# Mixture-of-experts layer with gathered conditioning: a low part on Pool, ranks ahead of a transpose, half a batch of the shared projection kept for later, and the last rows split over two engines

## What is computed

```python
h  = einsum('bsi,bio->bso', x, W[id]) + b[id][:, None, :]     # per batch its own 256x256 matrix
y  = (silu(h @ sw1) * (h @ sw3)) @ sw2                        # shared expert, 352 wide
scores = softmax(h @ gate_w)                                  # 8 experts, the best 2 kept
for e in range(8):                                            # routed experts, 176 wide
    y += weight[:, e] * ((silu(h @ rw1[e]) * (h @ rw3[e])) @ rw2[e])
return x + y
```

## Time and profile before

| | us |
|---|---|
| median of 3 runs | 119.95 (119.51 to 120.24) |
| the profiled execution's own time | 120.04 |
| its span in the profile | 118.4 |
| PE busy | 106.3 |
| DVE busy | 67.8 |
| ACT busy | 52.2 |
| Pool busy | 46.1 |

### The profile page before, as it was taken

The page is one execution under the profiler, slowest core; times in us unless marked ns, Lnnn a source line. Parts: engine busy times, 40 slices in busy tenths (PEclk is TensorE's granted clock), DMA queues, the critical chain, the costliest instruction groups (busy, mean ns, idle before and its releaser), DMA issues.

```text
span 118.4 us, 2226 instructions
## 1 busy us (share of the span) xinstructions
PE 106.3 (90%) x624; PEld 90.0 (76%) x624; DVE 67.8 (57%) x221; ACT 52.2 (44%) x131; POOL 46.1 (39%) x62
## 2 busy tenths in 40 slices
PE   6887997706999999899999999999999999999791
PEld 4676886404678888667799989999999997888570
DVE  1044575037984199867878676577655543024951
ACT  4035575117161693255657755346555655103000
POOL 4360077730776200001653443443453635704400
PEclk9999999965699999999999999999999999999999
DMA  3899999998886257131223343241012110029843
GB/s 72 237 298 276 345 352 371 383 324 226 216 194 235 89 158 201 41 96 48 91 95 106 100 130 119 86 136 59 29 44 83 50 67 21 0 55 383 329 184 118
DMA packets 16737, 19.08 MB, mean 161 GB/s; under 512 B 2338, under 2 KB 13718, under 8 KB 16726
## 3 DMA queue, kind: packets, MB, share of 16 engines
q1 hardware_dynamic: 13302, 12.62, 35.5%
q0 software_dynamic: 1984, 4.46, 10.7%
q10 hardware_dynamic: 1440, 1.86, 4.7%
HBM read 12.64 MB, written 7.21 MB: 168 GB/s over the span
## 4 chain that ended last, share of the span: by engine, by line
PE 73%; DMA 8%; issue 6%; another core or an unknown queue 3%; POOL 3%; DVE 2%; ACTq 1%; ACT 1%; POOLq 1%; DVEq 0%
PE bank L846 52%; DMA y_area<-_out_by_choice_and_token 6%; PE bank L858 6%; PE bank L978 4%; PE bank L1013 4%; DMA _out_by_choice_and_token<-y_area,dest 2%; PE bank L876 2%; PE bank L873 1%; ACTq L306 1%; POOL _out_by_choice_and_token L406 1%; PE bank L875 1%; POOLq L287 1%; POOL cond_area L288 1%; POOL ids_bc L365 1%
## 5 line engine op out<-in xcount | busy, mean ns | idle before, releaser
L406 POOL DMA_INDIRECT _out_by_choice_and_token<-y_area,dest x23 | 23.6, 1025 | 40.7 <-DVE y_area L767 26.4
L394 POOL DMA_INDIRECT rows_by_expert<-h_area,slot x16 | 15.5, 971 | 15.9 <-DVE slot L628 11.6
L846 PE MATMUL bank<-w_all,hsT_hi 128*128 x72 | 21.6, 342 | 0.0
L846 PE MATMUL bank<-hT_area,sh_area 128*128 128x512 f32 (+1 forms) x72 | 18.7, 421 | 0.0
L846 PEld LDWEIGHTS bank<-hT_area,sh_area 128*128 128x128 f32 (+1 forms) x72 | 13.7, 193 | 4.2
L846 PEld LDWEIGHTS bank<-w_all,hsT_hi 128*128 128x128 f32 x72 | 13.0, 188 | 0.0
L761 DVE TENSOR_TENSOR y_area<-y_area,bank 128x176 f32<-128x176 f32 x23 | 7.7, 335 | 8.5 <-ACT y_area L503 4.3
L503 ACT ACTIVATE y_area<-bank 128x176 f32<-128x176 f32 x23 | 7.3, 318 | 10.1 <-PE bank L846 8.2
L846 PE MATMUL bank<-w_all,hsT_lo 128*128 x36 | 11.5, 320 | 0.0
L846 PE MATMUL bank<-raw,gT_f 88*128 x44 | 11.3, 378 | 0.0
L546 DVE TENSOR_TENSOR hsT_lo<-bank,hsT_hi 128x256 fp32r<-128x256 f32 x18 | 7.6, 423 | 6.3 <-ACT hsT_hi L499 5.5
(11 more groups left out here) (128 smaller groups left out, 198.2 us busy)
## 6 DMA issues: line engine op xcount, KB each, us to landing
h_area<-rows_by_expert SPq DMA_DIRECT2D x23, 128.0 KB
raw<-in_L_ffn_rw_dram SPq DMA_DIRECT2D x16, 176.0 KB
raw<-in_L_ffn_rw_dram SPq DMA_DIRECT2D x2, 704.0 KB
rows_by_expert<-x_area SPq DMA_DIRECT2D x8, 128.0 KB
y_area<-_out_by_choice_and_token SPq DMA_DIRECT2D x4, 256.0 KB, 4.4
y_area<-_out_by_choice_and_token ACTq DMA_DIRECT2D x4, 256.0 KB, 5.1
out_dram<-x_area SPq DMA_DIRECT2D x3, 256.0 KB, 2.1
sh_raw<-in_L_ffn_sw_dram SPq DMA_DIRECT2D x2, 352.0 KB, 5.0
```

The costliest lines, as they stand in the source:

```text
L394: nc.gpsimd.indirect_dma_start(out=rows_dram, out_offset=bass.IndirectOffsetOnAxis(ap=slot[:, i, t:t + 1], axis=0), in_=h_sb[:, t, :], in_ ...
L406: nc.gpsimd.indirect_dma_start(out=y_dram, out_offset=bass.IndirectOffsetOnAxis(ap=dest[:, j:j + 1], axis=0), in_=y_sb[j % NBY], in_offset ...
L846: last = nc.tensor.matmul(dst, w, v, start=start and n == 0, stop=stop and n == len(operands) - 1)
```

## The change

- Pool makes the low part of the shared weights' first column block (96 columns of four slices, 128 partitions) between `dispatch(0)` and `dispatch(1)`; DVE no longer does. The semaphore is split in two (`sh_lo_pool`, `sh_lo_dve`).
- `ranks(0)` stands on PE ahead of the wait for `biasT_ready` and the transposes of the last batch (`turn_x(3)`).
- Only `shared_down(0, 0)` comes ahead of the tiles; `shared_down(0, 1)` comes after the last tile, into the upper half of bank 5. `base_of` of batch 0 is two half-size adds, one ahead of the tiles and one behind.
- `WARM_BEFORE_ROWS` is 6 instead of 18.
- Of the last batch, tile `j` = 0 is finished by DVE alone (two `weigh`), tile `j` = 1 by PE and DVE as before; two diagonal matrices are no longer made.

```diff
-WARM_BEFORE_ROWS = 18
+WARM_BEFORE_ROWS = 6
...
-        y_acc = [bank[1], bank[4], bank[7], bank[6]]
+        y_acc = [[bank[1][:, 0:D], bank[5][:, D:2 * D]]] + [[bank[n][:, 0:D], bank[n][:, D:2 * D]] for n in (4, 7, 6)]
+        acc_ps = [None] + [bank[n][:, :] for n in (4, 7, 6)]
...
-            for b in range(B):
+            dispatch(0)
+            pool.wait_ge(sh_hi_ready, 1)
+            nc.gpsimd.tensor_tensor(sh_lo[:, :, shared_cols(0)], sh_raw[:, :, shared_cols(0)],
+                                    sh_hi[:, :, shared_cols(0)].bitcast(F32), ALU.subtract).then_inc(sh_lo_pool, 1)
+            for b in range(1, B):
                 dispatch(b)
...
-            def base_of(b):
-                dve.wait_ge(acc_ready, b + 1)
-                x_row = x_sb[:, b].rearrange("p j d -> p (j d)")
-                nc.vector.tensor_tensor(x_row, y_acc[b][:, :], x_row, ALU.add).then_inc(base_ready, 1)
+            def base_of(b, j):
+                dve.wait_ge(acc_ready, JS * b + j + 1)
+                nc.vector.tensor_tensor(x_sb[:, b, j, :], y_acc[b][j], x_sb[:, b, j, :], ALU.add).then_inc(base_ready, 1)
...
-            sh_lo_of(0)
...
-            base_of(0)
+            base_of(0, 0)
...
-            base_of(1)
+            base_of(0, 1)
+            dve.wait_ge(acc_ready, JS * BH)
+            x_row = x_sb[:, 1].rearrange("p j d -> p (j d)")
+            nc.vector.tensor_tensor(x_row, acc_ps[1], x_row, ALU.add).then_inc(base_ready, 1)
...
-                    dve.wait_ge(weighed_ready, JS * (b - BH) + j + 1)
+                    if b == B - 1 and j == 0:
+                        dve.wait_ge(y_in[b], 16 * TOPK)
+                        for i in range(TOPK):
+                            weigh(b, i, j)
+                        continue
+                    dve.wait_ge(weighed_ready, min(JS * (b - BH) + j + 1, JS + 1))
...
+            ranks(0)
             pe.wait_ge(biasT_ready, 1)
             turn_x(3)
-            ranks(0)
...
             table()
-            for j in range(JS):
-                shared_down(0, j)
+            shared_down(0, 0)
             turn_rows(0)
...
+            shared_down(0, 1)
             for b in range(1, B):
                 for j in range(JS):
                     shared_down(b, j)
...
-                for j in range(JS):
+                for j in range(1 if b == B - 1 else 0, JS):
                     add_products(weighed_ps[b - BH][j], [(diagonal[b - BH][j][i][:, :], y_tok[:, b, i, j * D:(j + 1) * D])
```

More of the change, by code:

```diff
@@ L232, in adaln_moe_ffn @@
         sh_hi_ready = sem("sh_hi_ready")
-        sh_lo_ready = sem("sh_lo_ready")
+        sh_lo_pool = sem("sh_lo_pool")
+        sh_lo_dve = sem("sh_lo_dve")
         htok_ready = sem("htok_ready")
@@ L534, in _ @@
             for b in range(BH, B):
-                act.wait_ge(acc_ready, b + 1)
-                nc.scalar.copy(acc_sb[b - BH][:, :], y_acc[b][:, :]).then_inc(acc_sb_ready, 1)
+                act.wait_ge(acc_ready, JS * (b + 1))
+                nc.scalar.copy(acc_sb[b - BH][:, :], acc_ps[b]).then_inc(acc_sb_ready, 1)
         @block.vector
@@ L632, in sh_lo_of @@
                 dve.wait_ge(sh_hi_ready, c + 1)
-                lo_part(sh_lo[:, :, cols], sh_raw[:, :, cols], sh_hi[:, :, cols]).then_inc(sh_lo_ready, 1)
+                lo_part(sh_lo[:, :, cols], sh_raw[:, :, cols], sh_hi[:, :, cols]).then_inc(sh_lo_dve, 1)
             def at_row_of(first, last):
@@ L798, in _ @@
                     w2_lo_of(s - 2)
-                if E + 4 <= s < E + 4 + NT // 2:
+                if E + 4 <= s < E + 4 + NT // 2 and s - E - 4 + NT // 2 != JS * (B - 1):
                     diagonals_of(s - E - 4 + NT // 2)
-            base_of(1)
+            base_of(0, 1)
+            dve.wait_ge(acc_ready, JS * BH)
+            x_row = x_sb[:, 1].rearrange("p j d -> p (j d)")
+            nc.vector.tensor_tensor(x_row, acc_ps[1], x_row, ALU.add).then_inc(base_ready, 1)
             def weigh(b, i, j):
@@ L806, in weigh @@
                 if i == 1:
-                    dve.wait_ge(combining, t + 1)
+                    dve.wait_ge(combining, min(t, JS * BH) + 1)
                 nc.vector.scalar_tensor_tensor(
@@ L815, in _ @@
                 if b == 0:
-                    dve.wait_ge(base_ready, BH)
+                    dve.wait_ge(base_ready, JS + 1)
                 for i in range(TOPK):
@@ L883, in shared_up @@
                 if w == 0:
-                    pe.wait_ge(sh_lo_ready, c + 1)
+                    if c == 0:
+                        pe.wait_ge(sh_lo_pool, 1)
+                    else:
+                        pe.wait_ge(sh_lo_dve, c)
                 if g < 3:
@@ L900, in shared_down @@
                 toks = slice(b * S + j * P, b * S + (j + 1) * P)
-                last = add_products(y_acc[b][:, j * D:(j + 1) * D],
+                last = add_products(y_acc[b][j],
                                     [(gated[0:shared_rows(c), c, toks], sh2_raw[0:shared_rows(c), c, :])
                                      for c in range(NSH)], True, True)
-                if j == JS - 1:
-                    last.then_inc(acc_ready, 1)
+                last.then_inc(acc_ready, 1)
             def ranks(part):
@@ L1062, in _ @@
             pe.wait_ge(late_y_ready, NTILE - FIRST_DOWN)
-            pe.wait_ge(diagonal_ready, TOPK * JS * (B - BH))
+            pe.wait_ge(diagonal_ready, TOPK * (JS * (B - BH) - 1))
             keep_warm(WARM_BEFORE_ROWS)
```

## The result

| | before | after |
|---|---|---|
| median | 119.74 us (119.51 to 120.24, 4 runs) | 115.17 us (114.82 to 115.61, 4 runs) |
| the profiled execution's own time | 120.04 | 114.82 |
| its span | 118.4 | 113.2 |
| mean granted clock of PE | 0.971 | 0.985 |

The ratio is 0.9599, with the interval 0.9552 to 0.9646: 4.0% faster. The direction was right, the size was not. Of the 5.2 us that the span lost, 4.5 had been gained by the time the first weighted add starts, and 0.7 behind it.

A forecast was written before the change was run, and what follows sets the result against it. PE was taken to bound the tile loop, but not the two ends. From the profiled 120.04 us, 1.35 (shared down), 0.60 (last rows) and 0 (front) gave 118.09, so 118.0 for the median, range 116.8 to 119.5.

The forecast's parts named there:

- First term: Ahead of the tile loop: six shared down products fewer on PE bring the loop and all behind it 1.35 us earlier.
- hidden anyway: Before the loop: the last shared gate or other DVE work sets `up(0)`, leaving only the tail's 0.6; 119.4 us, chance 0.09.
- base add: Before tile 0's gate: DVE's half-wide base add ends at 49.5, ahead of the gate due at 49.82.
- Second term: Last rows: sharing them between DVE and PE ends the last add 0.80 us earlier, worth 0.6 us, ends 0.0 and 0.8.
- that rival: At the end: with 6 fillers PE meets the last rows at clock 0.50; 119.9 us, chance 0.04.
- Third term: Front: Pool's low part and earlier `ranks(0)` are worth 0 while PE's wait keeps its length; bounds −4.8 and +1.4 us.
- standstill: Front: PE stands still from 22.84 to 27.67, waiting for `both` from DVE, whose logit reductions are released late.
- my tolerance: Sign at the front: the third part's ranks start at 27.7 within 0.4; over 1 us away means the front's forecast was wrong.
- the standstill shrinks: Front: less traffic between 20 and 21 us shortens PE's wait by one step of 1.4 us; 116.7 us, chance 0.10.
- lower bound of −4.8 us: Front: the case that PE's wait ahead of the third part's ranks vanishes, worth −4.8 us.

The follow-up runs named there:

- after_c: The changed kernel run again, against the kernel before on chip 4: 114.90 us beside 120.71, ratio 0.9512.
- half_only: Kernel before with only half of batch 0's shared down projection moved behind the tiles and 6 fillers (chip 1): 118.98 us, ratio 0.9864.
- last_only: Kernel before with only the last tile rows shared by PE and DVE, 18 fillers kept (chip 1): 120.24 us, ratio 0.9976.
- ranks_only: Kernel before with only batch 0's ranks moved ahead of the last batch's transposes (chip 1): 120.03 us, ratio 0.9972.
- no_pool_c: The whole change with the low part back on DVE, against the kernel before on chip 4: 118.69 us, ratio 0.9880.
- pool_only: Kernel before with only the low part moved to Pool, ahead of batch 1's scatters (chip 1): 117.37 us, ratio 0.9738.
- pool_dummy_c: Kernel before, DVE keeping its low part, Pool subtracting as many unused elements ahead of batch 1's scatters (chip 4): 117.95 us, ratio 0.9755.
- hold_batch1_b: Kernel before with Pool holding batch 1's scatters until the third part is cast, no work added (chip 3): 113.66 us, ratio 1.0024.
- no_pool_dummy: The whole change with the low part on DVE and an unused subtraction on Pool, against the kernel before (chip 5): 114.09 us, ratio 0.9878.

## Why the prediction was wrong, step by step

**First term (1.35 us, shared down halved): right alone, a third of it kept in the change.** Alone it gave 1.6 us (0.9864; interval 1.0 to 2.3 us). In the change itself the stretch from the table's start to the first expert product went from 49.27 − 45.13 = 4.14 us to 44.70 − 41.01 = 3.69, only 0.45 less: six records take 1.56 us instead of twelve in 2.69 (1.13 less), PE waits 0.61 us before `shared_down(0, 0)`, for a gate behind ACT's late silu, and the transposes and ACT's copy take 0.07 more. The rival "hidden anyway" thus had two thirds of it here, by another gate than it named. The `up(0)` itself was released by ACT's copy, as forecast. That the base add ends in time held as well.

**Second term (0.6 us, last rows): right in the profile.** The last add stands 0.88 us closer to the first weighted add (forecast 0.80), and 0.72 of it reaches the end of the span (forecast 0.6). Both Pool adds fall on weighted adds: eight took 5.28 us where 7 · 0.40 + 0.47 = 3.27 are due, a price of 2.0 us, forecast 2.10. Timed alone it gave 0.3 us, which these runs don't tell from 0.6 or from zero. The clock at the end stayed full; that rival is out.

**Third term (0, the front): wrong; this is the step that failed.** The sentence was "All this is worth 0 as long as the standstill keeps its length", and the choice of 0 out of −4.8 to +1.4 was made because "the eight fills and the weights that saturate the DMA are issued by SP and are not touched". The ranks of the third part came 3.02 us early, three times my tolerance, though those fills and weights were as they had been and the DMA as full. An operation of Pool ahead of batch 1's scatters, which I had weighed only by its traffic ("0.5 MB of some 2.5 MB"), was enough.

What the 3.02 are made of: PE's idle 4.83 us ahead of the ranks are gone. Of these, 0.98 come back because `shared_up` starts later, and 1.03 because its six records run at the clock of 0.50 (2.58 us against 1.55); 0.20 is won by modelled ends that overlap, since the ranks now start before the six records end: 4.83 − 0.98 − 1.03 + 0.20 = 3.02. The 0.98 hang on another sentence of the third term, that "ACT takes them up before its next product is due". ACT took up the last batch at 20.12 instead of 19.13, and PE waited 1.92 us instead of 0.71.

The term also put the clock at nothing. Before, the windows have 0.50 from about 24.8 us, inside the standstill, to about 31.7; now from 22.5 to about 25.9, so PE does some 4.0 us of work at that clock before and 3.4 now. From the ranks to the table it takes 45.13 − 27.67 = 17.46 us before and 41.01 − 24.65 = 16.36 now, 1.10 less, behind the ranks; ahead of them 1.03 was lost. In sum the clock gave next to nothing back. So the sum goes: 3.02 at the ranks, 1.10 to the table and 0.45 to the first product make 4.57; 0.09 is lost in the loop and its reads, 0.72 gained at the end: 5.2 in the span, against 1.95 forecast.

For Pool's start on another sort of work the prediction took up to 0.9 us, which no run shows: the gaps on either side of the low part were 0.03 and 0.16 us.

**The rival "the standstill shrinks" had the sign and the place, at one step of 1.4 us and a chance of 0.10.** The lower bound of −4.8 us stood in the text, but the range was cut at 116.8. A wait of 4.8 us that I could not explain, directly on PE's path, should have widened the range to at least half of it.

**What the standstill is.** Shown: it is made of releases that reach VectorE or ACT 1 to 5 us after PE's product. It is there on chips 1 and 4 and not on 2, 3 and 5, at the same DMA share. An operation of Pool ahead of batch 1's scatters, with a use (chips 1 and 4) or without one (chip 4), removes PE's long wait ahead of the third part's ranks (batch 1's scatters start 0.5 to 1.2 us later by it); late releases remain, on instructions that PE needs less soon.

Only fitted to the rows: in eight of nine profiles a late release comes 1.0 to 1.7 us after Pool's fourth scatter of batch 1 ends. It fits as well to the end of the stretch in which the DMA is full: the column "DMA full until" has the end of the last quarter of a microsecond, up to 27 us, with a share of 0.95 or more, and in the same eight the release comes 0.05 to 0.8 us after it. A second stretch tells the two apart. Behind Pool's last scatter, that of batch 3, a gate of VectorE (in after and after_c a silu of ACT) is late again, by 1.5 to 1.9 us after the scatter's end, and there the DMA share of the microsecond before it was 0.64 or less.

| kernel | 4th scatter of batch 1 ends | late instruction starts | DMA full until | last scatter ends | late instruction starts |
|---|---|---|---|---|---|
| before | 24.75 | 26.31 (logits) | 25.75 | 39.35 | 41.14 |
| half_only | 24.69 | 26.32 (logits) | 26.25 | 39.27 | 41.09 |
| last_only | 24.72 | 26.37 (logits) | 26.25 | 39.40 | 41.13 |
| ranks_only | 25.09 | 26.17 (logits) | 25.75 | 39.00 | 40.79 |
| no_pool_c | 24.31 | 25.80 (logits) | 25.75 | 38.76 | 40.36 |
| after | 25.23 | 26.28 (rank sums) | 26.00 | 37.44 | 38.97 |
| after_c | 25.20 | 26.27 (rank sums) | 25.50 | 37.37 | 38.86 |
| pool_only | 25.92 | 27.07 (rank sums) | 27.00 | 38.35 | 39.96 |
| pool_dummy_c | 25.59 | 25.01 (rank sums), not so | 25.75, not so | 36.05 | 37.99 |

So a full DMA is not needed for a late release; a run of scatters stands ahead of each release in the table but one. In the profiles of chips 2, 3 and 5 with the same scatters none of these instructions is late. The fit has its gaps: other late releases come between two scatters (ACT's at 38.13 in the kernel before) or 0.9 us after one (ACT's at 20.12 in the changed kernel). And the thought that Pool's operation opens a gap (19.25 to 20.44 in the changed kernel) through which the logits pass doesn't meet the rows: they are read at 21.03 to 22.48, while the next scatters run. The run that delays the scatters without an operation met no chip with the standstill, so whether the delay or the operation counts stays open, as does the cause in the hardware.

## What to carry to other kernels

An idle stretch whose releaser the profile can't name, at saturated DMA, is not a constant of the kernel: a microsecond in another engine's queue can move it off the critical path. The low clock doesn't simply go with it: here a new, shorter wait in front brought 3.4 us of work at half clock where there had been 4.0. Price such a stretch with both bounds in the range, and look at which late release the critical engine waits for at once. And try a change of this sort on more than one chip: its main gain (3.7% of 4.9%) was there where the kernel before took 120 us, and nothing was left of it where it took 113.7.

## What the hardware showed that was not expected

- Five chips fell in two groups for one and the same kernel: 120.5 and 120.7 us, or 113.5, 113.7 and 113.9. Most executions on the slower ones show PE's clock at 0.97 on average, on the faster at 1.00. No profile of the kernel before on a faster chip was kept; in hold_batch1_b, which only adds a wait, the ranks start at 22.21 and the first expert product at 42.93, against 27.67 and 49.27: 6.3 of the 6.7 us between the spans (111.7 and 118.4) are made up ahead of the tile loop.
- What a collision of Pool's add with VectorE's weighted adds costs depends on who starts first. Now Pool's adds start at 103.81 and 106.40, inside weighted adds that began at 103.71 and 106.32 and have 0.4 us to go. Both Pool adds take 1.52 us, and the weighted adds behind them, from 104.11 and 106.72, take 1.49 and 1.48. Before, Pool's adds found VectorE idle (107.39) or 0.1 us from the end of its add (109.63) and took 1.27 and 1.26. The Trainium skill, page "SBUF — State Buffer", section "SBUF: two separate sides", says that of a GpSimd operation that reads SBUF and a VectorE operation with two SBUF inputs, the one that starts first has the shared ports for its whole instruction and the other blocks. These rows agree with it in both directions:

```profile
L815 DVE SCALAR_TENSOR_TENSOR x_area<-y_area,weight,x_area x10: 468/474/1491, 103.7 to 110.1; 128x256 f32<-128x256 f32 x10
```

- Pool's subtraction of 384 elements per partition took 1.00 us (forecast 0.95, from 512 in 1.27), and little time passed in going from scatters to it and back: gaps of 0.03 and 0.16 us. The unused one, with one tensor as both inputs, took 0.84 us in no_pool_dummy.
